# A gated cross-attention block: scores of a tile in one run, attention products of a tile in one run behind its turns, single normalised tiles

## The reference

```python
x = x + tanh(g_xattn[0]) * attention(layernorm(x), ctx, ctx, W_q, W_k, W_v, W_o, qpos, kpos, mask)
x = x + tanh(g_ffn[0]) * ffn(layernorm(x), W_r, W_k, W_v, mu_r, mu_k)

# attention, per head: softmax with 1 added to the sum
scores = Q @ K.T * scale - slope[h] * (qpos[:, None] - kpos[None, :])   # masked: -inf
e = exp(scores - max(scores)); attn = e / (1 + sum(e)); out = (attn @ V) @ W_o.T

# ffn
x_prev = x shifted by one token
xr, xk = mu_r * x + (1 - mu_r) * x_prev, mu_k * x + (1 - mu_k) * x_prev
out = sigmoid(xr @ W_r) * (square(relu(xk @ W_k)) @ W_v)
```

## Time and profile before

| | |
|---|---|
| median of 3 runs | 1525.86 us (1525.16 to 1526.19) |
| profiled execution, its span | 1519.6 us |
| PE busy, matmuls in flight | 1442.7 us (95%) |
| PEld busy, weight loads | 1083.1 us (71%) |
| DVE busy | 1161.5 us (76%) |
| ACT busy | 889.5 us (59%) |
| POOL busy | 721.3 us (47%) |
| mean granted clock of PE | 0.999 |

### The profile page before, as it was taken

The page is one execution under the profiler, slowest core; times in us unless marked ns, Lnnn a source line. Parts: engine busy times, 40 slices in busy tenths (PEclk is TensorE's granted clock), DMA queues, the critical chain, the costliest instruction groups (busy, mean ns, idle before and its releaser), DMA issues.

```text
span 1519.6 us, 32873 instructions
## 1 busy us (share of the span) xinstructions
PE 1442.7 (95%) x10864; PEld 1083.1 (71%) x10864; DVE 1161.5 (76%) x2889; ACT 889.5 (59%) x2928; POOL 721.3 (47%) x766
## 2 busy tenths in 40 slices
PE   7988899999999999999999999999999999999998
PEld 6876767677676767667686766767676676768667
DVE  4456868787887868798786879878687887868775
ACT  5147474665747465574747566473756657475662
POOL 0003455545455555545555464545546454555542
PEclk9999999999999999999999999999999999999999
DMA  8721001020200102020010202011020101001000
GB/s 270 215 66 49 8 29 50 0 76 0 56 20 28 49 0 76 0 56 20 28 49 14 62 0 56 20 36 41 14 62 0 56 20 53 23 27 50 1 30 28
DMA packets 53009, 65.95 MB, mean 43 GB/s; under 512 B 23024, under 2 KB 29168, under 8 KB 52976
## 3 DMA queue, kind: packets, MB, share of 16 engines
q1 hardware_dynamic: 52976, 65.52, 14.6%
HBM read 40.87 MB, written 24.64 MB: 43 GB/s over the span
## 4 chain that ended last, share of the span: by engine, by line
PE 48%; DVE 34%; issue 11%; ACT 3%; DMA 2%; DVEq 1%; SPq 0%; POOL 0%; ACTq 0%; POOLq 0%
PE rotating L401 33%; DVE probs L1038 7%; PE probs_bank L561 5%; DVE diff L1100 4%; PE score_bank L460 4%; DVE mix_k L1095 4%; PE attn_bank L575 3%; DVE relu L1100 3%; DVE square L1095 2%; PE score_bank L401 2%; ACT probs L773 2%; DVE mask_in L1137 2%; DVE stats L1008 2%; DVE norm L1017 2%; DVE xs L1064 2%
## 5 line engine op out<-in xcount | busy, mean ns | idle before, releaser
L773 ACT ACTIVATE probs<-probs,neg_max 128x120 f32<-128x120 f32 x1024 | 391.2, 385 | 29.6 <-DVE neg_max L1042 29.6
L1320 POOL TENSOR_TENSOR probs<-probs,recip 128x960 f32<-128x960 f32 x128 | 229.7, 1794 | 237.5 <-DVE recip L1053 237.5
L401 PE MATMUL rotating<-mixed_key,w_key 128*128 128x512 f32 x720 | 205.0, 413 | 24.8 <-ACT gated L825 24.8
L401 PE MATMUL rotating<-w_proj,attn_t 128*128 128x512 f32 x768 | 220.9, 417 | 2.9 <-DVE xnt_or_act L1023 2.0
L781 ACT COPY probs_t<-probs_bank 120x512 f32<-120x512 f32 x256 | 149.8, 585 | 121.3 <-PE probs_bank L561 121.1
L1038 DVE SCALAR_TENSOR_TENSOR probs<-mask_in,score_bank 128x120 f32<-128x120 f32 x1024 | 213.0, 269 | 9.5 <-PE score_bank L460 9.5
L401 PE MATMUL rotating<-w_value,xnt_or_act 128*128 128x512 f32 x720 | 202.3, 409 | 10.2 <-DVE xs L1064 10.2
L401 PE MATMUL rotating<-w_gate,mixed_gate 128*128 128x512 f32 x768 | 209.7, 409 | 0.0
L401 PE MATMUL rotating<-xnt_or_act,w_query 128*128 128x256 f32 x1536 | 198.7, 286 | 0.5 <-DVE xnt_or_act L1023 0.5
L773 ACT ACTIVATION_READ_ACCUMULATOR probs<-probs,neg_max 128x1 f32 x1024 | 194.0, 189 | 0.0
L401 PEld LDWEIGHTS rotating<-xnt_or_act,w_query 128*128 128x128 f32 x1536 | 187.7, 191 | 1.9 <-DVE xnt_or_act L1023 0.8
(11 more groups left out here) (126 smaller groups left out, 2167.7 us busy)
## 6 DMA issues: line engine op xcount, KB each, us to landing
xs<-in_x_dram SPq DMA_DIRECT2D x64, 256.0 KB, 2.9
out_dram<-gated SPq DMA_DIRECT2D x64, 256.0 KB, 3.0
value_scratch<-gated SPq DMA_DIRECT2D x16, 240.0 KB, 2.6
mask_in<-in_mask_dram SPq DMA_DIRECT2D x16, 240.0 KB, 2.6
keys_t<-key_scratch SPq DMA_DIRECT2D x16, 240.0 KB, 3.6
values<-value_scratch SPq DMA_DIRECT2D x16, 240.0 KB, 3.8
probs<-in_ctx_t_dram SPq DMA_DIRECT2D x6, 480.0 KB, 7.0
key_scratch<-query_t SPq DMA_DIRECT2D x12, 240.0 KB, 5.1
```

What stands on the lines that cost most here:

```text
L401: mm = pe.matmul(bank, stationary(a, c), moving(b, c), start=(i == 0), stop=(i == MATMULS - 1))
L773: e = act.activation(probs[:, t % 2, head, :], probs[:, t % 2, head, :], ACT.Exp, bias=neg_max[:, t % 2, head:head + 1], accum_out=sums[:, ...
L1320: pool.tensor_tensor(part, part, recip[:, t % 2, heads].unsqueeze(2).to_broadcast((P, H // 2, NK)), ALU.mult)\
```

## The change

The scores of a tile stand in one run ahead of the products that they were mixed with. In the attention of a tile, a turn stands ahead of each four of twelve products; behind the fourth turn stand four products of the next tile in order, then all four groups of attend, then the other eight products. So value 0 goes between the turns of tile 1, where value 1 was, and value 1 around its attend; in tile 3 turn1 1 and the first four products of value 3 come ahead of attend. probs_t gets four buffers, one for each group. norm1 and norm2 become one tile each (for the first batch norm1 alternates with norm2). The lists of ACT, DVE, POOL and SP stay as they are.

```diff
-        norm1 = sb("norm1", [P, 2, D])
-        norm2 = sb("norm2", [P, 2, D])
+        norm1 = sb("norm1", [P, D])
+        norm2 = sb("norm2", [P, D])
...
-        probs_t = sb("probs_t", [NK, 2, J, P])
+        probs_t = sb("probs_t", [NK, G, J, P])
...
             def attend(b, t, g):
-                pe.wait_ge(probs_t_ready, (b * QT + t) * G + g + 1)
                 if g == 0:
+                    pe.wait_ge(probs_t_ready, (b * QT + t + 1) * G)
...
-                def with_scores(t, what, tile, portions):
-                    at = 0
+                def all_scores(t):
                     for g in range(G):
                         scores(b, t, g)
-                        use(what, tile, range(at, at + portions[g]))
-                        at += portions[g]
-
-                def with_attention(t, what, tile, portions=(4, 3, 3, 2)):
-                    at = 0
+
+                def with_attention(t, beside, after_turns):
                     for g in range(G):
                         turn_probs(b, t, g)
-                        use(what, tile, range(at, at + portions[g]))
-                        at += portions[g]
-                        if g > 0:
-                            attend(b, t, g - 1)
-                    attend(b, t, G - 1)
-
-                with_scores(0, "gate", 0, (3, 3, 3, 3))
+                        if g < G - 1:
+                            use(*beside, range(4 * g, 4 * g + 4))
+                    if after_turns == ("value", 3):
+                        use("turn1", 1)
+                    use(*after_turns, range(4))
+                    for g in range(G):
+                        attend(b, t, g)
+                    use(*after_turns, range(4, MATMULS))
+
+                all_scores(0)
+                use("gate", 0)
                 use("gate", 1)
                 use("key", 0)
-                with_scores(1, "key", 1, (3, 3, 3, 3))
-                with_attention(0, "key", 2)
-                use("key", 3)
-                with_scores(2, "proj", 0, (3, 3, 3, 3))
-                use("value", 0)
-                with_attention(1, "value", 1)
-                with_scores(3, "gate", 2, (4, 4, 4, 0))
+                all_scores(1)
+                use("key", 1)
+                with_attention(0, ("key", 2), ("key", 3))
+                all_scores(2)
+                use("proj", 0)
+                with_attention(1, ("value", 0), ("value", 1))
+                all_scores(3)
+                use("gate", 2)
                 use("turn2", 0)
                 use("proj", 1)
-                with_attention(2, "value", 2)
-                use("gate", 3)
+                with_attention(2, ("value", 2), ("gate", 3))
                 use("turn1", 0)
                 use("turn2", 1)
-                with_attention(3, "proj", 2)
-                use("turn1", 1)
-                use("value", 3)
+                with_attention(3, ("proj", 2), ("value", 3))
                 use("proj", 3)
...
             def normalise1(b, t):
                 dve.wait_ge(rstd1_ready, b * QT + t + 1)
-                if earlier(b, t, 2):
-                    dve.wait_ge(done["turn1"], b * QT + t - 1)
...
+                else:
+                    dve.wait_ge(done["turn1"], b * QT + t)
+                    place = norm1
...
             def normalise2(b, t):
                 dve.wait_ge(rstd2_ready, b * QT + t + 1)
-                if earlier(b, t, 2):
-                    dve.wait_ge(done["turn2"], b * QT + t - 1)
+                if earlier(b, t, 1):
+                    dve.wait_ge(done["turn2"], b * QT + t)
```

More of the change, by code:

```diff
@@ L133, in flamingo_block @@
         tail_relus = [relu, square]
-        tail_squares = [norm1[:, i] for i in range(2)]
+        tail_squares = [norm1[:], norm2[:]]
+        first_norms = [norm1, norm2]
         wk_split = mixed_key
@@ L481, in turn1 @@
                 pe.wait_ge(norm1_ready, b * QT + t + 1)
+                place = first_norms[t % 2] if isinstance(b, int) and b == 0 else norm1
                 for c in range(CT):
                     channels = slice(c * P, (c + 1) * P)
-                    mm = pe.transpose(bank_of["turn1", t][:, channels], norm1[:, t % 2, channels], ident[:])
+                    mm = pe.transpose(bank_of["turn1", t][:, channels], place[:, channels], ident[:])
                 return mm
@@ L490, in turn2 @@
                     channels = slice(c * P, (c + 1) * P)
-                    mm = pe.transpose(bank_of["turn2", t][:, channels], norm2[:, t % 2, channels], ident[:])
+                    mm = pe.transpose(bank_of["turn2", t][:, channels], norm2[:, channels], ident[:])
                 return mm
@@ L575, in attend @@
                     mm = pe.matmul(attn_bank[j * HD:(j + 1) * HD, g * P:(g + 1) * P],
-                                   values[:, head * HD:(head + 1) * HD], probs_t[:, g % 2, j, :],
+                                   values[:, head * HD:(head + 1) * HD], probs_t[:, g, j, :],
                                    start=True, stop=True, skip_group_check=True)
@@ L780, in probs_out @@
                 act.wait_ge(probs_turned, (b * QT + t) * G + g + 1)
-                act.copy(probs_t[:, g % 2], probs_bank[0:NK, :].rearrange("k (j q) -> k j q", j=J))\
+                act.copy(probs_t[:, g], probs_bank[0:NK, :].rearrange("k (j q) -> k j q", j=J))\
                     .then_inc(probs_t_ready, 1)
@@ L1014, in normalise1 @@
                 dve.wait_ge(rstd1_ready, b * QT + t + 1)
-                if earlier(b, t, 2):
-                    dve.wait_ge(done["turn1"], b * QT + t - 1)
-                dve.tensor_scalar(norm1[:, t % 2], x_tile(b, t), mv1[:, t, 0:1], rstd1[:, t:t + 1], ALU.subtract, ALU.mult)\
+                if isinstance(b, int) and b == 0:
+                    if t >= 2:
+                        dve.wait_ge(done["turn1"], t - 1)
+                    place = first_norms[t % 2]
+                else:
+                    dve.wait_ge(done["turn1"], b * QT + t)
+                    place = norm1
+                dve.tensor_scalar(place[:], x_tile(b, t), mv1[:, t, 0:1], rstd1[:, t:t + 1], ALU.subtract, ALU.mult)\
                     .then_inc(norm1_ready, 1)
@@ L1082, in normalise2 @@
                 dve.wait_ge(rstd2_ready, b * QT + t + 1)
-                if earlier(b, t, 2):
-                    dve.wait_ge(done["turn2"], b * QT + t - 1)
-                dve.tensor_scalar(norm2[:, t % 2], x_tile(b, t), mv2[:, 0:1], rstd2[:], ALU.subtract, ALU.mult)\
+                if earlier(b, t, 1):
+                    dve.wait_ge(done["turn2"], b * QT + t)
+                dve.tensor_scalar(norm2[:], x_tile(b, t), mv2[:, 0:1], rstd2[:], ALU.subtract, ALU.mult)\
                     .then_inc(norm2_ready, 1)
```

## The result

| | before | after |
|---|---|---|
| median | 1525.51 us (1523.22 to 1526.19) | 1562.94 us (1558.51 to 1564.89) |
| profiled execution, its span | 1519.6 us | 1556.7 us |
| mean granted clock of PE | 0.999 | 0.967 |
| batch in the loop, mean of 14 | 87.84 us | 90.57 us |

The changed kernel is slower: 1.0248 times the time before, 95% interval 1.0229 to 1.0266. A batch is measured from one batch's distances on DVE (the first step of the position bias) to the next batch's. The 14 batches of the loop account for 14 x 2.73 = 38.2 us; what lies before them is 2.87 shorter and what lies behind them 1.74 longer, and 38.2 - 2.87 + 1.74 = 37.1 is the difference of the spans. In every run listed the time is 1.8 us above the span; the rest of the 6.3 us between span and median is that the profiled execution of before was a short one.

What follows compares the result with a forecast made beforehand. PE, DVE and ACT were taken to bound the kernel in series, not PE alone. Waits of 28, outer batches 1 and clock 12 gave +41 us on the median of 1525.9, so 1567 us, range 1546 to 1590.

Steps and rivals of the forecast that it cites:

- Tile 0 of the attention: Turn 3 stays put behind an ACT copy, attn_out(0) is 0.9 us late; key 0 waits about 3 us.
- Tile 1: PE waits some 3.5 us for POOL with value 0 undone; DVE's stretch gains only 0.2 us.
- Tile 3: Attention stands behind value 3's first products: attn_low(3) 3.0 us late, 2.2 at the mixing; less 0.2, 2.0 a batch.
- The step that failed: In tile 3, residual(2) on DVE would move by no more than tile 1's 0.2 us.
- the waits alone: Loss without the clock: 2.0 us a batch, 28 over 14; as a rival with no clock fall, 1555 us, chance 0.25.
- The clock: PE's clock falls behind long idle stretches; 1.7 us at one place in every second batch, 12 us in all.
- The idle stretch of nearly 3 us in tile 3: PE idle there, broken by a turn, in every batch; a slow clock behind it would be on the path.
- The outer batches: Batch 0 (no value 3 in that place) and the last (no next x): 1 us for both together.
- clock in every batch: Rival: one fall at tile 1 each batch, 1579 us; at tile 3 as well up to 1603; chance 0.20.
- PE gains: Rival: POOL and ACT deliver tiles 0 and 1 earlier, DVE starts 3.8 us earlier, -1.6 a batch: 1504 us; chance 0.07.
- PE is the bound: Rival: PE's 95% busy time is the limit, so 15 x 7.6 = 114 us go: 1412 us; chance 0.03.

Runs made afterwards that it cites:

- e8: e3 plus eight products whose result nobody reads, ahead of turn1 1 in tile 3: 1553.03 us, 1.0200 of before.
- after (both times): The changed kernel, and the same kernel unaltered measured a second time beside e9: 1562.94 us, then 1567.17 us (1.0284 of before).
- e1: The changed kernel with tile 3's attention put back as before: 1538.79 us, 1.0106 of before.
- e2: The changed kernel plus twelve products whose result nobody reads, ahead of tile 1's first turn: 1539.98 us, 1.0109 of before.
- e5: The changed kernel with both edits, e1's (tile 3's attention as before) and e2's (twelve unread products): 1514.82 us, 0.9956 of before.
- e3: The changed kernel with tile 1 put back as before (value 0 ahead of the attention): 1567.67 us, 1.0310 of before.
- e4: The changed kernel with the attention of all four tiles as before; all scores in runs, single norms, four probs_t buffers kept: 1512.43 us, 0.9932 of before.
- e6: The kernel before with the single normalised tiles (norm1, norm2) and nothing else changed: 1526.58 us, 1.0024 of before.
- e9: The kernel before with only the scores of tiles 1 to 3 in runs; two norms, two probs_t buffers: 1512.43 us, 0.9926 of before.
- e7: e4 with tile 0's scores left mixed with gate 0, so only tiles 1 to 3 have runs: 1512.40 us, 0.9932 of before.

## Why the prediction was right, and where its sizes were off

The time, 1562.94, lies 4 below the forecast of 1567, and the mechanism is the one forecast. Two of its terms were mis-sized, in opposite directions.

- **Tile 0 of the attention.** Right: turn 3 did not move (21.34 against 21.36), attn_low(0) is late by 0.83 (0.9 forecast), key 0 waits 2.88 ("about 3").
- **Tile 1.** Right: a wait of 3.3 for POOL (3.5 forecast), and DVE's sums of tile 2 earlier by 0.26 (0.2 forecast) where the clock holds.
- **Tile 3.** Right in itself: attn_low(3) is 3.03 later behind residual(2) (3.0 forecast). At turn1_low 3 that is 80.26 - 78.96 + 0.82 = 2.1 against residual(2) in batch 4 (2.2 forecast).
- **The step that failed:** "DVE's time there comes from an unbroken queue since 746.81, so it doesn't move by more than the 0.2". It moved by 0.82 at residual(2). The second part of mix 0 takes 1.14 us in after; in before it took 1.94:

DVE in before, batch 7:

```profile
766.26 1.94 DVE L1100 SCALAR_TENSOR_TENSOR diff<-diff,mu,xn2t 128x128 f32<-128x128 f32 x4
```

The first and the third of its four instructions alone:

```profile
766.26 0.35 DVE L1100 SCALAR_TENSOR_TENSOR diff<-diff,mu,xn2t 128x128 f32<-128x128 f32 x1
...
766.79 1.14 DVE L1100 SCALAR_TENSOR_TENSOR diff<-diff,mu,xn2t 128x128 f32<-128x128 f32 x1
```

POOL in before, batch 7:

```profile
766.75 1.04 POOL L1341 TENSOR_TENSOR relu<-xn2t 128x512 f32<-128x512 f32 x1
```

POOL in after, batch 7, the same step and the one ahead of it:

```profile
781.37 0.28 POOL L1335 COPY xn2t<-xn2t 128x4 f32<-128x4 f32 x1 [0.48 <-ACT xn2t L800]
781.73 1.04 POOL L1348 TENSOR_TENSOR relu<-xn2t 128x512 f32<-128x512 f32 x1
```

Before, POOL's step lies inside DVE's, and the instruction that starts behind its start takes 1.14 instead of 0.35; after, it waits for ACT and starts when DVE's (780.72 + 1.14) is nearly over. That the gain hangs on tile 1's order is shown: the busy time of that group (its rows stand at e8) is 81.2 to 82.9 us in after (both times), e1, e2 and e5, and 90.7 to 91.6 in before, e3, e4 and e6 to e9, which have the old tile 1. That the overlap with POOL makes the 0.8 is read from the traces, since no run moved POOL's step alone, but from all 128 instructions of the group: in before the 61 that start while a POOL TENSOR_TENSOR of over 0.9 us runs take 1.13 to 1.38 us, and the other 67, 31 of them already under way when POOL starts, 0.34 to 0.35; in after there are 49 of the first kind and 79 of the second. Twelve fewer at 0.8 us each make up the 9.5 us between 90.7 and 81.2. The Trainium skill, "SBUF — State Buffer", section "Who interferes with whom", says that a DVE instruction with two inputs in SBUF contends with a GpSimd instruction that reads SBUF; the rows agree.

So the waits alone cost 88.93 or 89.12 less 87.84, 1.2 us a batch and not 2.0: 16.6 us over 14 batches where 28 stood.

- **The clock.** The price of a fall was right, 1.6 us in batch 7 and 1.2 to 1.6 in all but one (1.7 forecast), and the place, tile 1. How often was wrong: not every second batch but 12 of 14. Of the 38.2 us in the loop, 38.2 - 16.6 = 21.6 are left for it, where 12 stood; e2, which takes the fall away, gives back 23. The idle stretch of nearly 3 us in tile 3 was wrong too: in batch 7 it is 0.23 before turn1 1 and 0.94 before value 3. The clock fell there in batch 1 alone, where turn1 1 waited 1.16.
- **The outer batches** were put at +1 and are -1.1.

The sum on record was 28 + 1 + 12 = 41, and the spans show 16.6 + 21.6 - 1.1 = 37.1. The near hit is in part luck: the two errors, -11.4 and +9.6, almost cancel. How often the clock fell, the rival "clock in every batch" had better.

The experiments split it another way, by edits: 24 to 25 us for tile 3, 23 to 24 for the clock at tile 1, and a gain of some 9 (e5) in what is left. Its trace puts 4.5 of that in the loop and 5.2 ahead of it, so how much the runs of scores and the mixing bring is not shown. 25 + 23 - 9 = 39, near the measured 37.

- **PE gains** (1504) and **PE is the bound** (1412) did not happen: PE has 49 us less to do and POOL's and ACT's steps hold tiles 0 and 1 where they were. A part of "PE gains" is real, though, and was not seen: the runs of scores of tiles 1 to 3 are worth 11 us by themselves (e9, 0.74% of 1524.57), by the trace through tile 2's run, which no kernel tried alone. The prediction counted that run only inside tile 1's wait.
- **Why e3 missed.** It took the fall at tile 1 as tied to that wait alone. Putting tile 1 back lost the gain in the mixing too (91.5 - 81.2 = 10.3); turn1 1 then waits 1.62 for DVE and not 0.30 as in e2, and there the clock fell (14.6 us by e8). Together 25 of the 29; the rest is open.

## What to carry to other kernels

An engine that is busy for 95% of the span need not set the pace alone; here it lost 49 us of work and the kernel got slower. Ask of each edit which wait ends last behind it, and what else stands in the queue behind the instruction that waits. The products that filled another engine's latency were worth more there than packed together elsewhere; without them PE idled ahead of work on the path, its clock fell, and even useless products in that place were a gain. Try the parts of a change one by one: here the part that adds no wait on the path (scores in one run, attention as before) is 0.7% faster than the kernel before, while the whole is 2.5% slower.

## What the runs showed of the hardware that was not expected

- **The clock's fall moves to another idle place.** Behind the same wait of 3.3 us at tile 1 it fell in 12 of 14 batches of after and in all 14 of e1. Without that wait, in e3, it fell in tile 3 in 9 of 14, after idle stretches of 1.62 and 0.94 us with a turn between them; with 0.24 to 0.31 and 0.94 there, in e2, it fell in none of 13. Why it spares two batches of after and five of e3 is not shown.
- **A switch between scores and products costs PE time.** Four groups of scores, each followed by three products, take 4 x 1.32 = 5.28 us; the run and the twelve products take 3.90 by the prediction's estimate, and 3.96 in after (tile 1 and key 1, from 729.27 to 733.23). The Trainium skill, "TensorEngine Tiling (Array Packing)", section "Key Properties", says that a change of tiling mode drains the engine; the 1.3 us agree, though no run shows that the drain is all of it. In e7 the first turn of tile 1 came 0.67 earlier, and the batch was 0.6 shorter.
- **Two engines in one memory.** In before and after, a DVE instruction of the same group that started while a POOL TENSOR_TENSOR of over 0.9 us ran took at least three times as long, 1.13 to 1.38 us instead of 0.34 to 0.35; one already under way when POOL started was not slowed. One such instruction fewer is the 0.8 us at residual(2) in batch 7; in e3, which has thirteen more of them than after, the group is busy for 10.3 us more.
